# Placing the head-masked low parts of the keys: eight small DMAs per half image in place of copies on GpSimd and VectorE

## The chip, the cores and the metric

One NeuronCore of one Trainium2 chip runs the whole kernel. The metric is the device time of one execution in microseconds (us), lower is better. Three runs of the kernel before gave 392.28, 393.44 and 391.3 us, median 392.28 us.

## The reference, cut to what matters

Eight images of 128 channels and 32x32 pixels go through a Swin-like block (layer norm, attention of 8 heads in windows of 8x8 = 64 tokens, projection, residual, layer norm, a 128-256-128 SiLU network, residual) and then through a linear attention without softmax, which the kernel folds into one 128x128 matrix per image.

```python
normed = _layernorm(win, ln1_g, ln1_b)
q, k, v = jnp.split(normed @ in_w.T + in_b, 3, axis=-1)      # 8 heads of 16
scores = jnp.einsum('bhsd,bhtd->bhst', q, k) / jnp.sqrt(16.)
o = jnp.einsum('bhst,bhtd->bhsd', softmax(scores), v)
win = win + o @ out_w.T + out_b
y = y + silu(_layernorm(y) @ fc1_w.T + fc1_b) @ fc2_w.T + fc2_b
out = wo @ (((wq x + bq) (wk x + bk) / N) (wv x + bv)) + bo + x
```

## The kernel before, in words

The work is cut into 16 half images of 512 tokens (8 windows, 4 pairs of windows), numbered from 0. `Loop.half(c)` is a half, `par` is its parity, and `h.n()` is the count that a semaphore has once half `h` has raised it. Five engine programs are written out by hand in a fixed order and meet only at semaphores. `images` lays them out: a prologue, image 0 (`step_even`, `step_odd`), a hardware loop over images 1 to 6, image 7, an epilogue. One step does the attention of half b (`b_*`), the layer norm and q, k, v of half b+1 (`a_*`), the projection, second layer norm and fc1 of half b-1 (`c_*`), fc2 of half b-2, and in every odd step the last 128x128 matrix of the image before (`d_*`). An engine does its own list strictly in order, so a wait holds all that is queued behind it.

Many products are made in three passes, for precision: a value is split into a high part of type float32r and a low part (the value less its high part), and high*high, high*low and low*high are summed. So q, k, and with them the operands of the scores, exist twice, as `q_h`, `q_l`, `k_h`, `k_l`.

Channels lie on the 128 partitions, 16 per head. The heads are kept apart by zeros: `qd_h` and `qd_l` hold q four times, each copy with the rows of two heads (32 partitions) and zeros elsewhere; `kd_h` and `kd_l` hold k twice, copy 0 with the rows of the even heads and copy 1 with those of the odd heads, zeros in the other rows. All have two slots, by parity.

- `spread_q` on SyncE (L346) fills `qd_h` and `qd_l` with four DMAs each (32 partitions, 2 KB a row); `spread_v` (L361) fills `vd` with four DMAs of 64 partitions and 256-byte runs. SyncE issues every DMA of the kernel, in order: `load_x`, `spread_q`, `spread_v` in each step, and the output at the end of an odd step. It waits for `q_high`, `q_low` and `v_kept` on the way. Zeros are laid once, in the prologue.
- `kd_h` is made on ScalarE (L894) as k_h times a 0/1 column `head_a`.
- `kd_l` is made the same way from `k_l`: copy 0 on GpSimd (`k_low_block`, L457), copy 1 on VectorE (`a_k_low_block`, L1148). As the product writes all 128 rows, no zeros are laid for it.
- TensorE: `b_score` (L611) makes the scores once with the high parts, for the row maxima alone; `b_scoreT` (L629 and L634) makes the transposed scores in three passes, minus the maxima. `b_scoreT(h, 0)` waits for `q_low_dma`, for both `kd_low` and for the widened maxima. `b_attn(h, 0)` (L649) waits for `v_dma`. In the prologue and first step the order of TensorE is: q, k, v of half 0, weights, score(0), score(1), scoreT(0), a_back, score(2), attn(0), q of half 1, scoreT(1), ...
- The next `k_l` (L1140) waits until the copies of the one before are done.
- GpSimd's prologue lays the identity, the zeros and ones of `vd` (L418, L422), then makes the reciprocal deviations of half 0 (L447, L449) on which VectorE's `normalise` (L1105) waits, then zeros of slot 1 of `qd` (L481, L482), then L457.

Of the kernel before, what the change touches and what calls it, by code (L numbers as in the profile page):

```python
# [34 lines left out]
F32 = mybir.dt.float32  # L35
# [87 lines left out]
def build(nc, x, ln1_g, ln1_b, in_w, in_b, out_w, out_b, ln2_g, ln2_b, fc1_w, fc1_b, fc2_w, fc2_b,  # L123
          wq, bq, wk, bk, wv, bv, wo, bo, out):
    ctx = ExitStack()
    with ctx:
# [117 lines left out]
        kd_high, kd_low = sems("kd_high", 2), sems("kd_low", 2)  # L244
# [59 lines left out]
        def _(sp):  # L304
# [55 lines left out]

            def spread_v(h):  # L361
# [17 lines left out]
            def prologue(loop):  # L379
                sp.wait_ge(q_zero_set[0], 2)  # L380
                spread_q(loop.half(0))
                sp.wait_ge(v_const_set, 5)
                spread_v(loop.half(0))
                sp.wait_ge(q_zero_set[1], 2)

            def step_even(loop, more, c):
                if more:
                    load_x(loop.half(2))
                spread_q(loop.half(1))
                spread_v(loop.half(1))  # L390

            def step_odd(loop, more, d):
                if more:
                    load_x(loop.half(3))
                    spread_q(loop.half(2))
                    spread_v(loop.half(2))
# [12 lines left out]
        def _(pool):  # L409
# [7 lines left out]

            pool.memset(vd[:], 0.0).then_inc(v_const_set, 1)  # L418
# [32 lines left out]
            def k_low_block(h):  # L451

                if h.follows(2):
                    pool.wait_ge(scoreT_ready[PAIRS - 1], h.n(2))
                pool.wait_ge(k_low, h.n())
                waited()
                pool.tensor_scalar(kd_l[:, h.par, :, 0, :], k_l[:].bitcast(F32).rearrange("p (win k) -> p win k", k=KEYS),  # L457
                                   head_a[:, 0:1], None, ALU.mult).then_inc(kd_low[0], 1)

# [19 lines left out]
            def prologue(loop):  # L479
# [3 lines left out]
                k_low_block(loop.half(0))  # L483
# [4 lines left out]
            def step(loop, b, with_a, with_next, with_c, with_tail, with_last=False):  # L488
# [5 lines left out]
                if with_a:  # L494
                    residual(a)
                    k_low_block(a)
# [26 lines left out]
        def _(pe):  # L523
# [92 lines left out]
            def b_scoreT(h, p):  # L616

                pe.wait_ge(max_wide_ready[p], h.n())
                if p == 0:
                    pe.wait_ge(q_low_dma, h.n(times=16 * QUADS))  # L620
                    pe.wait_ge(kd_low[0], h.n())
                    pe.wait_ge(kd_low[1], h.n())
# [409 lines left out]
        def _(dve):  # L1032
# [101 lines left out]
            def a_k(h):  # L1134
                dve.wait_ge(k_high, h.n())
                if h.follows(1):
                    dve.wait_ge(kd_low[0], h.n(1))
                if h.follows(1):
                    dve.wait_ge(kd_low[1], h.n(1))
                dve.scalar_tensor_tensor(k_l[:], p_a[1][:], qkv_b[:, 1:2], k_h[:].bitcast(F32),  # L1140
                                         ALU.add, ALU.subtract).then_inc(k_low, 1)

            def a_k_low_block(h):

                if h.follows(2):
                    dve.wait_ge(scoreT_ready[PAIRS - 1], h.n(2))
                dve.wait_ge(k_low, h.n())
                dve.tensor_scalar(kd_l[:, h.par, :, 1, :], k_l[:].bitcast(F32).rearrange("p (win k) -> p win k", k=KEYS),  # L1148
                                  head_a[:, 1:2], None, ALU.mult).then_inc(kd_low[1], 1)
# [117 lines left out]
            def prologue(loop):  # L1267
# [10 lines left out]
                a_k_low_block(a)  # L1278
# [5 lines left out]
            def step(loop, b, with_a, with_next, with_c, with_tail, with_d, with_last=False):  # L1284
# [47 lines left out]
                if with_a:  # L1332
                    a_k_low_block(a)
# [60 lines left out]
```

## Time and profile before

| | |
|---|---|
| runs | 392.28, 393.44, 391.3 us (median 392.28) |
| span of the profiled execution | 389.9 us, first to last instruction; what lies around it is not in the trace, and the median run stands 2.4 us above it |
| TensorE busy | 364.9 us, 94% |
| VectorE busy | 294.5 us, 76% |
| ScalarE busy | 241.8 us, 62% |
| GpSimd busy | 167.4 us, 43% |
| DMA | 31570 packets, 21.94 MB |
| one image in the loop | 44.1 us |

PE is TensorE's matmuls and PEld its weight loads, DVE is VectorE, ACT ScalarE, POOL GpSimd, SP SyncE; SPq rows are DMA issues. A busy PE includes pipelined matmuls that overlap, so it is not PE at its peak. The granted clock is shown as a share of full speed, 1.00 being 2.4 GHz and 0.50 being 1.2 GHz; at the very start, before the first record of the clock, the profile shows 1.00 whatever the matmuls' own durations say.

### The profile page before, as it was taken

How to read it: one execution, taken by the hardware profiler on the slowest of the kernel's cores; microseconds unless marked ns; L12 is line 12 of the kernel's file. 1: busy time of each engine (PE TensorE's matmuls, PEld its weight loads, DVE VectorE, ACT ScalarE, POOL GpSimd, SP SyncE). 2: the span in 40 equal slices, each digit the busy share in tenths (PEclk: the TensorE clock that was granted, in tenths of full speed). 3: DMA queues.
4: the chain of work that ended last, by engine and by line, in shares of the span. 5: the costliest groups of instructions: out<-in, count | busy, mean ns of one | idle time of the engine just before them, and what ended most of it. 6: DMA issues, size and time to landing. Idle time of an engine off the chain costs nothing. (4 is left out here: it accounts for less than half of the span.)

```text
span 389.9 us, 9822 instructions
## 1 busy us (share of the span) xinstructions
PE 364.9 (94%) x3349; PEld 312.5 (80%) x3349; DVE 294.5 (76%) x863; ACT 241.8 (62%) x438; POOL 167.4 (43%) x176
## 2 busy tenths in 40 slices
PE   3679999999999999999999999999999999999874
PEld 2467888888898888888888888888888888888663
DVE  8387888797688768797688868787688868676452
ACT  1426676764959477774958467674858467663540
POOL 6353154454364434544464434544455434441420
PEclk9999999999999999999999999999999999999796
DMA  4223030303222221303122121403122120300101
GB/s 121 40 77 97 23 100 11 102 0 82 73 63 52 49 58 59 102 0 81 58 77 54 46 62 54 108 0 78 57 74 61 40 67 29 79 6 10 45 1 54
DMA packets 31570, 21.94 MB, mean 56 GB/s; under 512 B 22272, under 2 KB 23360, under 8 KB 31552
## 3 DMA queue, kind: packets, MB, share of 16 engines
q1 hardware_dynamic: 31552, 21.71, 20.4%
q8 instruction: 10, 0.16, 0.2%
q14 instruction: 8, 0.07, 0.1%
HBM read 4.92 MB, written 4.19 MB: 23 GB/s over the span
## 5 line engine op out<-in xcount | busy, mean ns | idle before, releaser
L649 PEld LDWEIGHTS p_attn<-vd,probs 128*64 128x64 f32 x1024 | 52.7, 139 | 22.3 <-issue 15.1
L649 PE MATMUL p_attn<-vd,probs 128*64 128x34 f32 x1024 | 62.1, 244 | 2.8 <-ACT probs L910 2.8
L910 ACT ACTIVATE probs<-p_scoreT 128x512 f32<-128x512 f32 x64 | 38.6, 603 | 38.0 <-PE p_scoreT L634 37.5
L465 POOL TENSOR_TENSOR hid_l<-hid,hid_h 128x512 fp32r<-128x512 f32 x30 | 40.4, 1367 | 47.9 <-ACT hid_h L944 45.8
L611 PE MATMUL p_score<-kd_h,qd_h 128*128 128x128 f32 (+1 forms) x512 | 54.6, 249 | 0.8 <-DVE row_max L1158 0.8
L611 PEld LDWEIGHTS p_score<-kd_h,qd_h 128*128 128x128 f32 (+1 forms) x512 | 50.0, 163 | 5.0 <-DVE row_max L1158 1.3
L470 POOL TENSOR_TENSOR y_l<-y,y_h 128x512 fp32r<-128x512 f32 (+1 forms) x17 | 20.6, 1214 | 71.2 <-ACT y_h L924 71.2
L1158 DVE TENSOR_REDUCE row_max<-p_score 128x8 f32<-128x512 f32 x64 | 44.0, 688 | 6.6 <-PE p_score L611 6.6
L634 PE MATMUL p_scoreT<-qd_h,kd_h 128*128 128x256 f32 x128 | 41.3, 322 | 0.0
L457 POOL TENSOR_SCALAR kd_l<-k_l,head_a 128x512 fp32r<-128x512 f32 x16 | 26.7, 1669 | 33.8 <-DVE k_l L1140 20.0
L449 POOL TENSOR_TENSOR rstd<-rstd,minus_half 128x4 f32<-128x4 f32 (+1 forms) x33 | 35.5, 1075 | 2.8
L634 PE MATMUL p_scoreT<-qd_h,kd_l 128*128 128x256 f32 x128 | 36.1, 282 | 0.0
L634 PE MATMUL p_scoreT<-qd_l,kd_h 128*128 128x256 f32 x128 | 36.0, 282 | 0.0
L1105 DVE TENSOR_SCALAR xn_tok<-p_a,mv,rstd 128x128 f32<-128x128 f32 x64 | 21.9, 405 | 13.2 <-POOL rstd L449 13.1
L447 POOL TENSOR_SCALAR rstd<-mv 128x4 f32<-128x4 f32 (+1 forms) x33 | 7.6, 231 | 56.0 <-DVE mv L1097 56.0
L436 POOL TENSOR_SCALAR x_res<-x_in,out_b 128x256 f32<-128x256 f32 x32 | 29.6, 934 | 0.0
L1169 DVE CAST max_wide<-row_max 128x512 bf16<-128x512 f32 x48 | 27.7, 578 | 1.1
L629 PE MATMUL p_scoreT<-neg_ident,max_wide 128*128 128x128 bf16 x256 | 25.2, 221 | 2.0 <-DVE max_wide L1169 2.0
L634 PEld LDWEIGHTS p_scoreT<-qd_l,kd_h 128*128 128x128 f32 x128 | 24.4, 190 | 0.0
L634 PEld LDWEIGHTS p_scoreT<-qd_h,kd_h 128*128 128x128 f32 x128 | 24.3, 190 | 0.0
L634 PEld LDWEIGHTS p_scoreT<-qd_h,kd_l 128*128 128x128 f32 x128 | 24.1, 189 | 0.0
L894 ACT ACTIVATE kd_h<-k_h,head_a 128x512 fp32r<-128x512 f32 x32 | 22.9, 718 | 1.7 <-ACT k_h L887 0.4
(183 smaller groups left out, 881.9 us busy)
## 6 DMA issues: line engine op xcount, KB each, us to landing
x_in<-in_x SPq DMA_DIRECT2D x16, 256.0 KB, 2.8
qd_h<-q_h SPq DMA_DIRECT2D x64, 64.0 KB, 2.0
qd_l<-q_l SPq DMA_DIRECT2D x64, 64.0 KB, 2.0
vd<-v_tok SPq DMA_DIRECT2D x64, 64.0 KB, 2.2
out<-out_sb SPq DMA_DIRECT2D x16, 256.0 KB, 2.0
fc_rows<-in_L_conv_fc_w SPq DMA_DIRECT2D x2, 128.0 KB, 2.6
in_w_rows<-in_L_conv_in_w SPq DMA_DIRECT2D x1, 192.0 KB, 2.7
out_w_rows<-in_L_conv_out_w SPq DMA_DIRECT2D x1, 64.0 KB, 2.5
```

Of the source, the lines that this page charges most:

```text
L436: last = pool.tensor_scalar(in_windows(x_res[:, h.par, :], v), in_rows(x_in[:, h.par, :], v), out_b2[:, 0:1], None, ALU.add)
L449: pool.tensor_tensor(out_[:, tiles], out_[:, tiles], minus_half[:, tiles], ALU.pow).then_inc(out_set, 1)
L457: pool.tensor_scalar(kd_l[:, h.par, :, 0, :], k_l[:].bitcast(F32).rearrange("p (win k) -> p win k", k=KEYS), head_a[:, 0:1], None, ALU.mul ...
L465: pool.tensor_tensor(hid_l[:, t], hid[:, t], hid_h[:, t].bitcast(F32), ALU.subtract).then_inc(hid_low[t], 1)
L611: last = pe.matmul(p_score[0:rows, 2 * KEYS * j:2 * KEYS * (j + 1)], qd_h[:, h.par, j, 2 * KEYS * p:2 * KEYS * p + rows], kd_h[:, h.par, 2 ...
L629: pe.matmul(dst[:, :, j, :], max_wide[:, p % 2, 2 * j:2 * j + 2, :], neg_ident[:], start=j == 0, stop=False, skip_group_check=True)
L634: last = pe.matmul(dst[:, win], kd[:, h.par, window], qd[:, h.par, :, KEYS * window:KEYS * (window + 1)], start=False, stop=win == 1 and k ...
L649: last = pe.matmul(p_attn[64 * win:64 * win + 64, 2 * VB * j:2 * VB * (j + 1)], probs[:, p % 2, win, j, :], vd[:, h.par, 2 * p + win, :, : ...
L894: act.activation(kd_h[:, h.par, :, a, :], k_h[:].bitcast(F32).rearrange("p (win k) -> p win k", k=KEYS), ACT.Copy, scale=head_a[:, a:a + 1 ...
L910: act.activation(probs[:, p % 2], p_scoreT[:].rearrange("row (win j q) -> row win j q", win=2, j=QUADS), ACT.Exp, scale=SCORE_SCALE).then_ ...
L1158: dve.tensor_reduce(row_max[:, p % 2], p_score[:].rearrange("row (h k) -> row h k", h=HEADS), AXIS_X, ALU.max).then_inc(max_ready[p], 1)
L1169: dve.tensor_copy(max_wide[:, p % 2], row_max[:, p % 2].unsqueeze(2).to_broadcast([128, HEADS, KEYS])).then_inc(max_wide_ready[p], 1)
```

## The change

Both halves of `kd_l` are now written by SyncE's DMAs. A new function `spread_k_low` issues one DMA per head, 16 partitions each, from `k_l` to the head's copy of `kd_l`, eight per half image, between `spread_q` and `spread_v`. The two copies on GpSimd and VectorE and their semaphores go. Since the DMAs leave the rows of the other heads alone, GpSimd zeros all of `kd_l` once, at the start, ahead of the zeros of `vd`. TensorE waits for the eight DMAs in place of the two copies.

```diff
+            def spread_k_low(h):
+                sp.wait_ge(k_low, h.n())
+                if h.follows(2):
+                    sp.wait_ge(scoreT_ready[PAIRS - 1], h.n(2))
+                for head in range(HEADS):
+                    rows = slice(DH * head, DH * head + DH)
+                    sp.dma_start(kd_l[rows, h.par, :, head % 2, :].bitcast(F32),
+                                 k_l[rows, :].bitcast(F32).rearrange("p (win k) -> p win k", k=KEYS)
+                                 ).then_inc(kd_low_dma, 16)
...
                 spread_q(loop.half(0))
+                sp.wait_ge(kd_zero_set, 1)
+                spread_k_low(loop.half(0))
                 sp.wait_ge(v_const_set, 5)
                 spread_v(loop.half(0))
...
                 spread_q(loop.half(1))
+                spread_k_low(loop.half(1))
                 spread_v(loop.half(1))
...
                     spread_q(loop.half(2))
+                    spread_k_low(loop.half(2))
                     spread_v(loop.half(2))
...
+            pool.memset(kd_l[:].bitcast(F32), 0.0).then_inc(kd_zero_set, 1)
             pool.memset(vd[:], 0.0).then_inc(v_const_set, 1)
...
-            def k_low_block(h):
...
-                pool.tensor_scalar(kd_l[:, h.par, :, 0, :], k_l[:].bitcast(F32).rearrange("p (win k) -> p win k", k=KEYS),
-                                   head_a[:, 0:1], None, ALU.mult).then_inc(kd_low[0], 1)
...
                     pe.wait_ge(q_low_dma, h.n(times=16 * QUADS))
-                    pe.wait_ge(kd_low[0], h.n())
-                    pe.wait_ge(kd_low[1], h.n())
+                    pe.wait_ge(kd_low_dma, h.n(times=16 * HEADS))
...
                 if h.follows(1):
-                    dve.wait_ge(kd_low[0], h.n(1))
-                if h.follows(1):
-                    dve.wait_ge(kd_low[1], h.n(1))
+                    dve.wait_ge(kd_low_dma, h.n(1, times=16 * HEADS))
...
-            def a_k_low_block(h):
...
-                dve.tensor_scalar(kd_l[:, h.par, :, 1, :], k_l[:].bitcast(F32).rearrange("p (win k) -> p win k", k=KEYS),
-                                  head_a[:, 1:2], None, ALU.mult).then_inc(kd_low[1], 1)
```

The calls of `k_low_block` (GpSimd's prologue and step) and of `a_k_low_block` (VectorE's prologue and step) go with them.

## Rows read from the trace of the kernel before

**Rows 1.** Busy by stretch: us, PE, PEld, DVE, ACT, POOL, clock, DMA share, GB/s.
```profile
188.00:232.00 44.00, 43.76 (x415) 37.86 (x414) 34.95 (x105) 30.06 (x55) 20.41 (x20) 1.00 0.22 59
```
**Rows 2.** Lines L457 and L1148, the two copies: duration in ns, minimum, median, maximum.
```profile
L457 POOL TENSOR_SCALAR kd_l<-k_l,head_a x16: 1567/1570/1841, 17.5 to 335.5; 128x512 fp32r<-128x512 f32 x16
L1148 DVE TENSOR_SCALAR kd_l<-k_l,head_a x16: 476/477/488, 17.3 to 338.6; 128x512 fp32r<-128x512 f32 x16
```
**Rows 3.** Timeline, even step of image 4: start, duration, engine, line, operation, [idle before <-releaser].
```profile
203.73 2.66 SPq L369 DMA_DIRECT2D vd<-v_tok  x4
...
206.87 0.48 DVE L1148 TENSOR_SCALAR kd_l<-k_l,head_a 128x512 fp32r<-128x512 f32 x1
...
208.28 1.37 DVE L1105 TENSOR_SCALAR xn_tok<-p_a,mv,rstd 128x128 f32<-128x128 f32 x4 [0.93 <-POOL rstd L449]
```
**Rows 4.** Timeline, the same halves in the next step, TensorE.
```profile
211.95 0.40 PE L629 MATMUL p_scoreT<-neg_ident,max_wide 128*128 128x128 bf16 x4 [0.24 <-DVE max_wide L1169]
...
215.81 0.97 PE L649 MATMUL p_attn<-vd,probs 128*64 128x34 f32 x16
```
**Rows 5.** Timeline of the prologue and first step, from SyncE's first spreads on.
```profile
16.56 0.75 DVE L1140 SCALAR_TENSOR_TENSOR k_l<-p_a,qkv_b,k_h 128x512 fp32r<-128x512 f32 x1 [0.44 <-ACT k_h L887]
...
17.95 2.49 SPq L358 DMA_DIRECT2D qd_l<-q_l  x4
...
20.54 2.70 SPq L369 DMA_DIRECT2D vd<-v_tok  x4
...
22.12 0.91 PE L611 MATMUL p_score<-kd_h,qd_h 128*128 128x128 f32 x8 [0.78 <-DVE row_max L1158]
...
22.87 0.40 PE L629 MATMUL p_scoreT<-neg_ident,max_wide 128*128 128x128 bf16 x4
...
24.05 0.42 PEld L577 LDWEIGHTS p_a<-ident,xn_tok 128*128 128x128 f32 x4 [0.23 <-DVE xn_tok L1105]
...
26.50 0.97 PE L649 MATMUL p_attn<-vd,probs 128*64 128x34 f32 x16 [0.95 <-ACT probs L910]
```
**Rows 6.** DMA issues on the page: KB each, median us from issue to landing.
```profile
x_in<-in_x SPq DMA_DIRECT2D x16, 256.0 KB, 2.8
...
qd_l<-q_l SPq DMA_DIRECT2D x64, 64.0 KB, 2.0
vd<-v_tok SPq DMA_DIRECT2D x64, 64.0 KB, 2.2
```
**Rows 7.** Issue times in ns of line L320: minimum, median, maximum.
```profile
L320 SPq DMA_DIRECT2D x_in<-in_x x16: 334/386/547, 0.7 to 294.9; - x16
```
**Rows 8.** Timeline, half 1: SyncE in the first step, TensorE in the second.
```profile
34.17 2.65 SPq L369 DMA_DIRECT2D vd<-v_tok  x4
...
40.57 0.40 PE L629 MATMUL p_scoreT<-neg_ident,max_wide 128*128 128x128 bf16 x4
```
**Rows 9.** Timeline, half 15, the last: SyncE, then TensorE.
```profile
337.65 2.65 SPq L369 DMA_DIRECT2D vd<-v_tok  x4
...
344.21 0.40 PE L629 MATMUL p_scoreT<-neg_ident,max_wide 128*128 128x128 bf16 x4 [0.26 <-DVE max_wide L1169]
```
**Rows 10.** Timeline, GpSimd in the prologue.
```profile
2.09 1.91 POOL L418 MEMSET vd<- 128x2176 f32 x1
...
6.58 0.24 POOL L447 TENSOR_SCALAR rstd<-mv 128x4 f32<-128x4 f32 x1 [2.11 <-DVE mv L1097]
```
**Rows 11.** Granted clock by stretch near the end, columns as in the first group.
```profile
365.00:370.00 5.00, 4.54 (x14) 3.63 (x15) 2.14 (x8) 0.57 (x2) 2.76 (x4) 0.51 0.14 52
370.00:375.00 5.00, 4.13 (x28) 3.92 (x27) 3.83 (x8) 2.36 (x6) 1.28 (x2) 0.81 0.01 2
```
**Rows 12.** Timeline, TensorE before and within that stretch.
```profile
363.60 0.44 PE L665 MATMUL p_c<-ident,o_tok 128*128 128x128 f32 x2 [0.26 <-DVE o_tok L1180]
365.01 0.51 PE L529 MATMUL p_c<-o_h,wh 128*128 128x256 f32 x1 [0.98 <-ACT o_h L930]
...
367.75 0.63 PE L529 MATMUL p_c<-hid_l,wh 128*128 128x512 f32 x1
```

More of the change, by code:

```diff
@@ L243, in build @@
         q_high_dma, q_low_dma, v_dma = sem("q_high_dma"), sem("q_low_dma"), sem("v_dma")
-        kd_high, kd_low = sems("kd_high", 2), sems("kd_low", 2)
+        kd_high, kd_low_dma, kd_zero_set = sems("kd_high", 2), sem("kd_low_dma"), sem("kd_zero_set")
         score_ready, max_ready, max_wide_ready = sems("score_ready", 4), sems("max_ready", 4), sems("max_wide_ready", 4)
@@ L449, in rstd @@
                 pool.tensor_tensor(out_[:, tiles], out_[:, tiles], minus_half[:, tiles], ALU.pow).then_inc(out_set, 1)
-            def k_low_block(h):
[L453 to L456, printed above, removed]
-                pool.tensor_scalar(kd_l[:, h.par, :, 0, :], k_l[:].bitcast(F32).rearrange("p (win k) -> p win k", k=KEYS),
-                                   head_a[:, 0:1], None, ALU.mult).then_inc(kd_low[0], 1)
             def hidden_low(h, t):
@@ L482, in prologue @@
                 pool.memset(qd_l[:, 1].bitcast(F32), 0.0).then_inc(q_zero_set[1], 1)
-                k_low_block(loop.half(0))
                 rstd1_of(loop.half(1))
@@ L495, in step @@
                     residual(a)
-                    k_low_block(a)
                 if with_next:
@@ L1136, in a_k @@
                 if h.follows(1):
-                    dve.wait_ge(kd_low[0], h.n(1))
-                if h.follows(1):
-                    dve.wait_ge(kd_low[1], h.n(1))
+                    dve.wait_ge(kd_low_dma, h.n(1, times=16 * HEADS))
                 dve.scalar_tensor_tensor(k_l[:], p_a[1][:], qkv_b[:, 1:2], k_h[:].bitcast(F32),
                                          ALU.add, ALU.subtract).then_inc(k_low, 1)
-            def a_k_low_block(h):
-                if h.follows(2):
-                    dve.wait_ge(scoreT_ready[PAIRS - 1], h.n(2))
-                dve.wait_ge(k_low, h.n())
-                dve.tensor_scalar(kd_l[:, h.par, :, 1, :], k_l[:].bitcast(F32).rearrange("p (win k) -> p win k", k=KEYS),
-                                  head_a[:, 1:2], None, ALU.mult).then_inc(kd_low[1], 1)
             def b_max(h, p):
@@ L1277, in prologue @@
                 a_k(a)
-                a_k_low_block(a)
                 load_weights()
@@ L1331, in step @@
                 b_norm(b, 2)
-                if with_a:
-                    a_k_low_block(a)
                 if with_last:
```

## The prediction

> **What bounds the kernel now.** I read the busy time by stretch first. In one image of the loop TensorE is busy 43.76 of 44 us and no other engine over 35 [rows 1]. So in the loop an edit counts only if it makes TensorE do more or wait. The reader should then not look at what GpSimd and VectorE save, but at the time at which `kd_l` is complete against the time at which TensorE's scoreT(0) of that half wants it. For that I read the timeline, half by half: SyncE's queue on one side, L629 on the other. In the loop much of a step lies between them [rows 3, 4]; in the prologue there is no such distance, since half 0 is used as soon as it is made [rows 5].
>
> **Removed.** Sixteen copies of 1.57 us on GpSimd (25 us) and sixteen of 0.48 us on VectorE (7.6 us) [rows 2]. In a loop step the VectorE copy stands ahead of `xn_tok`, but VectorE still idles 0.93 us after it for GpSimd's rstd [rows 3], which is made from mv, and mv stands ahead of the copy in VectorE's order. So without the copies VectorE only waits longer, 0.93 + 0.48 us. Worth 0. A reason against a hidden gain is TensorE's 0.24 us of idle time per image [rows 1, 4]; all of it, seven times, would be 1.7 us.
>
> **Added on GpSimd.** One memset of 2048 words a partition, ahead of the 2176 of `vd` that took 1.91 us [rows 10]: 1.8 us. GpSimd had idled 2.11 us for VectorE's mv before rstd of half 0 [rows 10], so 0.3 us of cover are left; I take 0. Were it gone, each 0.1 us over would lengthen the prologue by as much.
>
> **Added on SyncE.** Eight DMAs per half between those of q_l and of v. The trace has no DMA of 16 partitions. Nearest in kind are `vd`'s, with 256-byte runs as here: four in 2.65 to 2.70 us, up to 0.68 each; those of q take four in 2.49, 0.62 each [rows 5, 8]. I take a pitch of 0.65, with 0.39 (x_in's issue [rows 7]) and 0.68 as ends. From issue to landing q takes 2.0 and v 2.2 us [rows 6]; half the bytes of either, so 2.1, ends 2.0 and 2.8 (x_in's). The eighth DMA of a half thus starts 7 x 0.65 = 4.55 us after the first and lands 6.65 us after it, and `vd`'s are issued 5.2 us later than now. Their share of the 16 engines is no limit: 0.22 is used in the loop [rows 1], by 12 spreads a half of 64 KB [rows 6] beside the loads and stores; eight of 32 KB add a third to the spreads.
>
> The Trainium skill speaks against this form of transfer: "DMA: Bandwidth & Descriptors", Rules for kernel authors, says that many small transfers should be coalesced and that under 64 KB one pays mostly overhead. The trace agrees so far as 64 KB in 2.0 us and 256 KB in 2.8 us show [rows 6]. The page's fit for one DMA on another issue path (2.0 us plus bytes over 436 GB/s) would put 32 KB at an estimated 2.1 us, the same as I took.
>
> **Where that meets TensorE, half by half.** The first of the new DMAs can go when q_l's are issued, which is where `vd`'s first stands now; k_l is there by then (in the prologue at 17.31 us [rows 5]).
> - Half 0: 20.54 + 6.65 = 27.2 us, and scoreT(0) began at 22.87 [rows 5]. TensorE waits 4.3 us more. Behind the wait stand a_back, score(2) and attn(0), and for them ScalarE's a_xn and VectorE's row maxima, so nothing fills it. Given back: a_back had waited 0.23 us for `xn_tok` [rows 5], which is early now. With the ends: 20.54 + 7 x 0.39 + 2.0 = 25.3, a wait of 2.4; or 20.54 + 7 x 0.68 + 2.8 = 28.1, a wait of 5.2. `vd`: first issue 25.74, fourth 27.8, landed 30.0; attn(0) would come at 26.50 + 4.1 = 30.6 [rows 5], so it is not held, by 0.6 us.
> - Half 1 (both sides shifted alike): 34.17 + 6.65 = 40.8 against 40.57 [rows 8]: 0.25 us, ends 0 and 1.2.
> - Even steps of the loop: 203.73 + 6.65 = 210.4 against 211.95: 1.5 us to spare. `vd` would land at 203.73 + 5.2 + 3 x 0.68 + 2.2 = 213.2 against 215.81: 2.6 to spare [rows 3, 4]. An odd step has the `d_*` work besides and leaves more room. Worth 0.
> - Half 15: 337.65 + 6.65 = 344.3 against 344.21 [rows 9]: 0.1 us, ends 0 and 1.1.
>
> **The clock.** TensorE would stand still from 22.12 + 0.91 = 23.0 [rows 5] to 27.2 us. In the trace of before its clock fell to the 1.2 GHz level at the end of the kernel, at a point where it had been idle for 0.98 us after a gap of 0.26: the stretch 365 to 370 has 0.51 and the next 0.81, so it was slow for some 7 us [rows 11, 12]. An idle time of four microseconds is far longer, so I expect the fall here, after which the first step's TensorE work runs at half pace until the clock is back. Seven slow microseconds do the work of 3.5: the cost has the ends 0 (no fall, or all under waits for ScalarE) and 3.5. I take 1.5, below the middle of the two, since about a microsecond of it lies under the wait for `probs` (0.95 us [rows 5]) and one case says little of how long the next spell is.
>
> The Trainium skill, "TensorE: Matmul & The Clock Gate", HAM oscillation, tells of the same: a wait for a DMA that is long enough puts the array back to half rate, and the next work starts cold. By that rule the fall is all but certain; the single case of rows 11 and 12 agrees.
>
> **The sum.** 4.3 - 0.2 + 1.5 + 0.25 + 0.1 = 5.95 us on a span of 389.9, so 395.8, and as the same 2.4 us lie around it, 392.28 + 5.95 = 398.2 us.
>
> **Rivals.**
> 1. The clock stays up or its fall is covered: 392.28 + 4.45 = 396.7 us. For it: the stage has other engines' waits to hide in, as 0.95 us before attn(0) [rows 5]. Against: rows 11 and 12.
> 2. The new DMAs go out faster, as x_in's do: the wait of half 0 is 2.4, halves 1 and 15 cost nothing, and so short a gap may leave the clock: 392.28 + 2.2 = 394.5. For it: x_in's 0.39 [rows 7]. Against: 256-byte runs cost 0.66 to 0.68 in the nearest rows [rows 5, 8].
> 3. The loop's even steps are late too, because a 16-partition DMA costs more than any seen, or lands late when eight are queued. It decides from a pitch of 0.65 + 1.5/7 = 0.87 us. At 1.0: 2.45 us more in half 0, half 1 and half 15, and 1.0 in each of 6 even steps: 398.2 + 7.4 + 6 = about 411.
> 4. The other side: faster. If a step's length were set by VectorE's chain and not by TensorE, the 0.48 us off VectorE in each half after the first [rows 2] would come back, 15 x 0.48 = 7.2 us, against the 5.95 lost: 391.0; with the 2.2 of rival 2 it is 387.3. It decides from 0.4 us per half. Against it: 43.76 of 44 busy [rows 1] and the 0.93 us of idle time right behind the copy [rows 3].
>
> That the change isn't what it says can be put aside: all five orders are written out by hand.
>
> **How the numbers follow.** Forecast with a fall of the clock 0.52 (its own range 396.5 to 400.5), rival 1 0.25, rival 2 0.10, rival 3 0.07, rival 4 0.06. Within 0.5% (2 us, about what a measurement of this kernel can tell from no change) lies half of rival 4 and some of rival 2's lower edge: 0.07. Faster by more: 0.04. Slower by more: 0.89. Range: from rival 2's 394.5 to 401.5, the forecast with a full fall of the clock (5.95 + 2 for the 3.5, and 1.3 for pitch and landing); rival 3 and rival 4 are left out.
>
> **What would show it.** In the timeline of the changed kernel L629 of half 0 starts at about 27.2 us, released by a DMA of `kd_l`; the eight issues take 5.2 us; if the clock fell, the matmuls of 512 columns (L529) that follow take 0.63 us each, as in the slow stretch [rows 12]; an image of the loop takes as long as before. I am wrong if the period of an image changes, if the issues have another pitch, or if scoreT(0) of a loop step waits for a DMA.

## The result: 401.3 us against 392.3, and where the 9 us lie

The changed kernel takes 401.31 us (median of 4 runs, 401.2 to 403.37), the kernel before 392.27 us beside it (391.3 to 393.44). The ratio is 1.0249, 95% interval 1.021 to 1.0287: slower by 9.0 us, where 5.95 were forecast. The profiled execution has a span of 399.6 us against 389.9, so 9.7 us are to be found between the two traces.

First the page of the changed kernel: its busy times, the wait of TensorE's transposed scores, and the new transfers.

```profile
PE 366.4 (92%) x3349; PEld 314.3 (79%) x3349; DVE 286.8 (72%) x847; ACT 242.1 (61%) x438; POOL 140.6 (35%) x161
...
DMA packets 50002, 26.15 MB, mean 65 GB/s; under 512 B 40704, under 2 KB 41792, under 8 KB 49984
...
L638 PE MATMUL p_scoreT<-qd_h,kd_l 128*128 128x256 f32 x128 | 36.3, 284 | 0.0
...
L633 PE MATMUL p_scoreT<-neg_ident,max_wide 128*128 128x128 bf16 x256 | 25.2, 221 | 9.2 <-DMA kd_l<-k_l 6.2
...
kd_l<-k_l SPq DMA_DIRECT2D x128, 32.0 KB, 2.1
```

GpSimd's busy time fell from 167.4 to 140.6 us and VectorE's from 294.5 to 286.8, for the most part the copies that are gone. It bought nothing. TensorE idles 9.2 us ahead of L633 (L629 before), 6.2 of them for `kd_l`. The same line's query says in how many places, and what an issue and a landing take (ns, then us):

```profile
L368 SPq DMA_DIRECT2D kd_l<-k_l x128: 599/600/1655, 20.6 to 349.8; - x128
...
  PE p_scoreT L633: 6.2, 3
...
DMA to landing us min/median/max: 2.1/2.1/3.1
```

Three waits, then, of 4.32, 1.46 and 0.44 us (halves 0, 1 and 2): 6.2 us, not 9.7. To find the rest I set the starts of TensorE's scoreT(p) of every half of the two traces side by side (64 pairs) and looked at where their distance grows. The timeline of the changed kernel, prologue and first step, answers [rows 5]:

```profile
20.56 5.19 SPq L368 DMA_DIRECT2D kd_l<-k_l  x8
22.15 0.90 PE L616 MATMUL p_score<-kd_h,qd_h 128*128 128x128 f32 x8 [0.79 <-DVE row_max L1152]
...
25.85 2.67 SPq L380 DMA_DIRECT2D vd<-v_tok  x4
27.37 0.59 PE L633 MATMUL p_scoreT<-neg_ident,max_wide 128*128 128x128 bf16 x4 [4.32 <-DMA kd_l<-k_l]
...
31.98 0.97 PE L653 MATMUL p_attn<-vd,probs 128*64 128x34 f32 x16 [0.90 <-ACT probs L914]
...
33.69 0.40 PE L633 MATMUL p_scoreT<-neg_ident,max_wide 128*128 128x128 bf16 x4
```

scoreT(0) went from 22.87 to 27.37 (+4.50), scoreT(1) from 28.20 to 33.69 (+5.49). The further microsecond is the clock, in the columns of [rows 1]; over the same 28 to 32 us the kernel before had 1.00:

```profile
24.00:28.00 4.00, 0.63 (x5) 0.66 (x6) 1.17 (x3) 0.00 (x0) 2.35 (x3) 0.50 0.29 59
28.00:32.00 4.00, 3.10 (x19) 2.95 (x18) 0.88 (x2) 1.77 (x6) 0.00 (x0) 0.67 0.41 115
```

Half 1 answers [rows 8]. SyncE is through with q_l 5.5 us later than before, as TensorE is with its work, but its eight issues take 6.20 us and not 5.19, and TensorE waits:

```profile
39.67 6.20 SPq L368 DMA_DIRECT2D kd_l<-k_l  x8
...
45.92 2.62 SPq L380 DMA_DIRECT2D vd<-v_tok  x4
47.61 0.38 PE L633 MATMUL p_scoreT<-neg_ident,max_wide 128*128 128x128 bf16 x4 [1.46 <-DMA kd_l<-k_l]
```

Half 2 is the first that the hardware loop uses. The kernel before, then the changed one:

```profile
51.80 3.29 SPq L369 DMA_DIRECT2D vd<-v_tok  x4
59.28 0.40 PE L629 MATMUL p_scoreT<-neg_ident,max_wide 128*128 128x128 bf16 x4 [0.25 <-DVE max_wide L1169]
```

```profile
58.76 5.60 SPq L368 DMA_DIRECT2D kd_l<-k_l  x8
66.06 0.38 PE L633 MATMUL p_scoreT<-neg_ident,max_wide 128*128 128x128 bf16 x4 [0.44 <-DMA kd_l<-k_l]
```

From SyncE's free place to TensorE's use there were 7.5 us here, where image 4 has 8.2 [rows 3, 4]. One of the eight issues took 1.07 us, and a loop step did wait for its DMAs.

Half 9, made in the even step of image 4 and used in the odd one, answers [rows 3, 4]:

```profile
211.03 5.15 SPq L368 DMA_DIRECT2D kd_l<-k_l  x8
...
215.47 1.37 DVE L1109 TENSOR_SCALAR xn_tok<-p_a,mv,rstd 128x128 f32<-128x128 f32 x4 [1.24 <-POOL rstd L465]
...
218.06 1.11 DVE L1163 CAST max_wide<-row_max 128x512 bf16<-128x512 f32 x1
219.41 0.38 PE L633 MATMUL p_scoreT<-neg_ident,max_wide 128*128 128x128 bf16 x4 [0.42 <-DVE max_wide L1163]
```

Here no DMA is waited for. VectorE's idle time before `xn_tok` grew from 0.93 to 1.24 us. But TensorE's wait for `max_wide` is 0.42 us where it was 0.24, though the CAST takes 1.11 us in both. That small difference comes back in every odd half of the loop. (In the even halves from 4 on TensorE has no such wait: for half 8 the CAST takes 0.43 us in both kernels and is done 0.3 us before its use. Half 2 is like the odd halves: the CAST took 1.12 us in the kernel before, and TensorE waited 0.25.) An image of the loop shows it in TensorE's busy time (43.76 before [rows 1]):

```profile
152.00:196.00 44.00, 43.58 (x412) 37.62 (x411) 34.21 (x102) 29.90 (x54) 16.75 (x18) 1.00 0.28 70
```

The account of the 9.7 us, by that distance (forecast terms beside it):

| where | measured | forecast |
|---|---|---|
| half 0, wait and clock | +5.47 | 4.3 - 0.2 + 1.5 |
| half 1 | +1.13 (1.57, of which 0.4 comes back within the step) | 0.25 |
| halves 2 to 15 | +1.31: 0.16 in half 2, 0.17 to 0.21 in each odd half from 3 to 13, 0.08 in half 15, nothing in the even ones from 4 on | 0.1 |
| behind scoreT(3) of half 15 | +1.76 (31.44 to 33.20 us) | 0 |

Half 0 came as forecast. The other three are what the experiments are about.

### The profile page after: what moved, and what is told of

It is laid out like the page before. It is cut to its first block and busy times, and to the rows that moved or that the text cites. A ratio compares the mean times of both kernels' runs of the same rounds, so it can differ in the third digit from the quotient of the medians.

```text
span 399.6 us, 9915 instructions
## 1 busy us (share of the span) xinstructions
PE 366.4 (92%) x3349; PEld 314.3 (79%) x3349; DVE 286.8 (72%) x847; ACT 242.1 (61%) x438; POOL 140.6 (35%) x161
## 5 line engine op out<-in xcount | busy, mean ns | idle before, releaser
L465 POOL TENSOR_TENSOR rstd<-rstd,minus_half 128x4 f32<-128x4 f32 (+1 forms) x33 | 33.7, 1021 | 2.8
L633 PE MATMUL p_scoreT<-neg_ident,max_wide 128*128 128x128 bf16 x256 | 25.2, 221 | 9.2 <-DMA kd_l<-k_l 6.2
L633 PEld LDWEIGHTS p_scoreT<-neg_ident,max_wide 128*128 128x128 bf16 x256 | 16.6, 98 | 15.0 <-issue 13.0
L1163 DVE CAST max_wide<-row_max 128x512 bf16<-128x512 f32 x48 | 25.9, 540 | 1.1
```

The source lines that it names most:

```text
L465: pool.tensor_tensor(out_[:, tiles], out_[:, tiles], minus_half[:, tiles], ALU.pow).then_inc(out_set, 1)
L633: pe.matmul(dst[:, :, j, :], max_wide[:, p % 2, 2 * j:2 * j + 2, :], neg_ident[:], start=j == 0, stop=False, skip_group_check=True)
L1163: dve.tensor_copy(max_wide[:, p % 2], row_max[:, p % 2].unsqueeze(2).to_broadcast([128, HEADS, KEYS])).then_inc(max_wide_ready[p], 1)
```

## The experiments

Each was timed beside the kernel before, on the same chip as it (its medians there 391.73 to 391.81 us). "Shift" is the distance of TensorE's scoreT(3) from that of the first trace of the kernel before; "end" is the time behind scoreT(3) of half 15, 31.44 us there.

### Half 0 and the clock

**Half 0 by the engines.** Theory: the eight DMAs of half 0 alone cost 5.5 us. GpSimd and VectorE make `kd_l` of half 0 as before, the DMAs all others.

```diff
                 spread_q(loop.half(0))
                 sp.wait_ge(kd_zero_set, 1)
-                spread_k_low(loop.half(0))
...
+                k_low_block(loop.half(0))
...
+                a_k_low_block(a)
```

> The changed kernel, but the low parts of half 0 alone are made by GpSimd and VectorE as before the change; the eight DMAs serve halves 1 to 15. Theory A (the largest part of the loss is the wait of TensorE for half 0's DMAs and the fall of its clock behind it, 5.5 us between scoreT(0) of half 0 and scoreT(1) of half 0 in the two traces): L629's first start returns to 22.9 us, the clock is not at 0.50 between 24 and 31 us, and the time is 401.3 - 5.5 = 395.8 us. Theory B (the loss is in the loop, by the added DMA traffic or by the waits on it, and what the prologue loses is made up later): no more than 1 us is gained, 400.3 us or more.

Measured: 393.9 us (10 runs), ratio 1.0068 (1.0038 to 1.0097), 7.4 us under the changed kernel. More than expected, for two reasons that the trace shows: half 1 adds nothing at scoreT(3), and the end is 0.49 us shorter than in the trace of before, 2.25 us shorter than in that of the changed kernel. The DMAs of half 1 are late here too: TensorE waits 0.32 us for them, which comes back within the half, since TensorE is 2.0 us later than before and SyncE only 0.9 (35.10 against 34.17). In half 2 it waits 0.63 us for them. Halves 2 and 3 add 0.39 and 0.32 us, the odd halves from 5 to 13 add 0.15 to 0.22. The half-0 shift is still 2.0: the clock fell in this execution too, though TensorE waited for no DMA:

```profile
28.00:32.00 4.00, 4.00 (x22) 3.40 (x23) 3.05 (x8) 1.29 (x2) 0.00 (x0) 0.57 0.09 22
```

**Both kernels once more.** How much of the half-0 shift belongs to the kernel, and how much to the execution? The two kernels unchanged, each profiled again.

> The kernel before, unchanged, for a second trace. Theory A (the end of the kernel behind scoreT(3) of half 15, 31.4 us in the first trace and 33.2 in the changed kernel's, differs from execution to execution with the places where the clock falls, and the 1.8 us are not the change's): the end is another length here, by half a microsecond or more, and the clock falls elsewhere. Theory B (the end is fixed for a kernel): 31.4 us again.

> The changed kernel, unchanged, for a second trace, with the same question as for the kernel before. Theory A: the end is not 33.2 us, and with it what half 0 loses to the clock (1.0 us in the first trace) may differ; scoreT(0) of half 0 starts at 27.4 us again, and each odd step is 0.17 us longer again. Theory B: 33.2 us again.

Measured: the kernel before, span 391.56 us (393.37 us), had a shift of 2.15 us in the first step, then nothing to the last half, and an end 0.44 us shorter (half a microsecond was asked of theory A). The changed one, span 399.59 (401.4 us), nearly repeated its first trace: shifts 5.46, 6.26 and 8.01 at halves 0, 1 and 15, end +1.69. Half 2 alone differs, 0.65 us in place of 0.16, with a wait of 0.92 us for its DMAs. The 2.15 us of the kernel before are the clock:

```profile
28.00:32.00 4.00, 4.00 (x23) 3.44 (x22) 3.08 (x8) 1.29 (x2) 0.00 (x0) 0.57 0.08 20
```

So the kernel before loses up to 2.15 us in its first step in some executions, and the trace that I predicted from was one without that loss. TensorE's longest wait there in this trace is the 0.95 us for `probs` before attn(0). Here the clock fell without a wait of four microseconds. The Trainium skill ("TensorE: Matmul & The Clock Gate", HAM oscillation) ties the fall to long waits for DMAs; that agrees with half 0 of the changed kernel, and does not describe this fall.

**Half 0 kept busy.** To price the clock alone: 32 matmuls into an unread bank stand ahead of scoreT(0) in the first step of the changed kernel, so that TensorE does not stand still. They are extra work, used by nothing.

```diff
+                if not with_c:
+                    for _ in range(32):
+                        pe.matmul(p_c[0][:, 0:2 * C], wh[:, 0, :], wh[:, 0:2, :], start=True, stop=True)
```

> The changed kernel with 32 matmuls of 256 columns more, on constant operands and into an unused bank, between score(1) and scoreT(0) of half 0, where TensorE waits for the DMAs. They fill 23.0 to 26.8 us at the full clock and delay nothing. Theory A (of the 5.5 us lost in half 0, 1.0 is the clock, which falls while TensorE waits): the granted clock stays 1.00 in the first step, scoreT(1) of half 0 follows scoreT(0) by 5.3 and not by 6.3 us, and about 1.0 us is gained, 400.3 us, if the end of the kernel doesn't change. Theory B (the 1.0 us is not the clock but the order of the work behind the wait): the distance stays 6.3 us and the time 401.3 us.

Measured: 401.39 us, ratio 1.024 (1.019 to 1.029): nothing gained, where 1.0 us was expected. The profiled execution shows what happened in it. The clock did stay up,

```profile
24.00:28.00 4.00, 3.30 (x28) 3.10 (x26) 1.52 (x4) 0.00 (x0) 2.71 (x3) 1.00 0.21 38
...
20.54 6.55 SPq L368 DMA_DIRECT2D kd_l<-k_l  x8
...
28.73 0.38 PE L633 MATMUL p_scoreT<-neg_ident,max_wide 128*128 128x128 bf16 x4 [1.43 <-DMA kd_l<-k_l]
```

and from scoreT(0) to scoreT(1) it took 5.08 us (28.73 to 33.81) instead of 6.32 in the changed kernel. The clock thus costs 1.24 us of half 0. But SyncE's eight issues took 6.55 us in this execution and scoreT(0) began 1.36 us later, which took it away. Whether that holds for the other three runs is not known. What follows from the trace: clock 1.2 us, wait 4.5, and a late DMA can eat the one if the other is won.

**Four of the eight from ScalarE.** If SyncE's issue pitch sets half 0, two queues halve it. ScalarE issues heads 4 to 7 of half 0.

```diff
-                for head in range(HEADS):
+                for head in range(HEADS if h.follows(1) else HEADS // 2):
...
+                for head in range(HEADS // 2, HEADS):
+                    rows = slice(DH * head, DH * head + DH)
+                    act.dma_start(kd_l[rows, 0, :, head % 2, :].bitcast(F32),
```

> The changed kernel, but of half 0's eight DMAs four are issued by ScalarE, idle at that time, and four by SyncE; halves 1 to 15 as in the change. Theory A (the wait of half 0 is the length of SyncE's queue, eight issues of 0.65 us, and a landing of 2.1): the last of them lands 4 x 0.65 = 2.6 us earlier, L629's first start is at 24.8 instead of 27.4 us, and as TensorE idles 1.8 us and no longer 4.3 the clock may stay up: 2.6 to 3.7 us gained, 397.6 to 398.8 us. Theory B (the sixteen DMA engines or the landing are the limit, not the issue): scoreT(0) starts at 27 us as before and the time is 401 us.

Measured: 398.01 us, ratio 1.0175 (1.0132 to 1.0219), 3.3 us under the changed kernel.

```profile
18.41 2.67 ACTq L979 DMA_DIRECT2D kd_l<-k_l  x4
20.80 2.61 SPq L368 DMA_DIRECT2D kd_l<-k_l  x4
...
25.05 0.43 PE L633 MATMUL p_scoreT<-neg_ident,max_wide 128*128 128x128 bf16 x4 [1.30 <-DMA kd_l<-k_l]
```

The wait of 4.32 us fell to 1.30 and scoreT(0) from +4.50 to +2.18. The two queues have about the same pitch (2.67 and 2.61 us for four); ScalarE starts 2.4 us before SyncE and is through 0.3 us after SyncE's first has started. The clock fell here too (0.66 in 24:28, 0.92 in 28:32), and the shift of half 0 is 3.0 us in place of 5.5. The profiled execution was the fastest of the four (396.16 us), and its end is 2.5 us shorter than in the changed kernel's trace (mean granted clock 0.88 against 0.79), so not all of the gain in time is the queue's.

### The DMAs or the wait: the rest of the loop

**The DMAs, read by nobody.** The kernel before, its copies kept, with the eight DMAs of each half added into a tile that nothing reads. It costs whatever SyncE's queue and the DMA engines cost, without TensorE's wait for `kd_l` (VectorE still waits for these DMAs before it writes the next `k_l`).

```diff
+        kd_x = sb("kd_x", [C, 2, WH, 2, KEYS], F32R)
...
+                    sp.dma_start(kd_x[rows, h.par, :, head % 2, :].bitcast(F32),
```

> The kernel before with the eight DMAs per half added at the same place of SyncE's order, but into a tile that nobody reads; kd_l is still made by GpSimd and VectorE and TensorE waits for these. It prices SyncE's queue alone. Theory A (the queue costs where what stands behind it is wanted at once): scoreT(0) of half 0 stays at 22.9 us, but the DMAs of v are issued 5.2 us later, so attn(0) of half 0 starts at about 30.1 instead of 26.5 us, with a fall of the clock behind it: 4 to 5 us in half 0, nothing in the loop: 396.5 to 398 us. Theory B (only the wait on kd_l costs): attn(0) is not held and the time is 392.3 to 393 us.

Measured: 395.75 us, ratio 1.0106 (1.0064 to 1.0148). From half 1 to half 15 the shift does not move, to 0.02 us: neither the queue, nor the packets, nor later `vd` cost the loop anything. All of the loss lies in half 0, +5.87 us, and there it is now `v` that is late, behind the eight issues. The time is only 4.0 us longer, and below the 396.5 expected, since the end of this execution is 1.85 us shorter than in the trace of before (mean granted clock 0.94 there against 0.77).

```profile
25.78 2.67 SPq L380 DMA_DIRECT2D vd<-v_tok  x4
...
30.14 1.50 PE L663 MATMUL p_attn<-vd,probs 128*64 128x34 f32 x16 [3.92 <-DMA vd<-v_tok]
```

**The copies, read by nobody.** The other side: the changed kernel with the 32 copies put back, into a tile that nothing reads.

```diff
+                pool.tensor_scalar(kd_x[:, h.par, :, 0, :], k_l[:].bitcast(F32).rearrange("p (win k) -> p win k", k=KEYS),
...
+                dve.tensor_scalar(kd_x[:, h.par, :, 1, :], k_l[:].bitcast(F32).rearrange("p (win k) -> p win k", k=KEYS),
```

> The changed kernel with the two copies put back on GpSimd and VectorE at their old places, into a tile that nobody reads: it prices what the change takes away. Theory A (the copies were hidden, as the prediction said): distances in the loop and time are the changed kernel's, 401.3 us within 1 us. Theory B (the copies cost something in each step, and the change loses in spite of a gain there): the loop is longer by up to 0.4 us a half, and the time goes to 403 us or more.

Measured: 400.28 us, ratio 1.0218 (1.0191 to 1.0244), 1.0 us under the changed kernel, within the spread of both. The whole time can't price the copies, since the clock differs in the trace: it stays low longer in the first step (0.70, 0.50 and 0.52 in 24:28, 28:32 and 32:36), which makes half 0 1.6 us longer than in the changed kernel, and the end is 29.80 us in place of 33.20 (mean granted clock 0.94 against 0.79). The loop is that of the changed kernel: 0.15 to 0.24 us in odd halves, 0.40 in half 2 (a wait of 0.65 us for its DMAs), 0 in the later even ones. So in the loop 25 us of GpSimd and 7.6 us of VectorE are worth nothing either way, as forecast.

```diff
+                kd_count = h.n(times=16 * HEADS) if p == 0 else None
...
-                    pe.wait_ge(kd_low_dma, h.n(times=16 * HEADS))
+                    pe.wait_ge(kd_low_dma, kd_count)
```

> The changed kernel, but TensorE's sequencer works out the count for its wait on the DMAs of kd_l ahead of the wait for the widened maxima, not behind it. Theory A (the 0.18 us by which each odd step of the loop is longer is this register operation, which stands between the wait for the maxima and the first weight load): the two traces' scoreT(0) keep their distance through the loop, the 0.18 us of halves 3, 5, ... 13 go, and 1.0 to 1.2 us are gained: 400.2 us. Theory B (the 0.18 us come of the DMAs themselves, by landing late or by their traffic): nothing changes, 401.3 us.

Measured: 400.79 us, ratio 1.0229 (1.0166 to 1.0293), odd halves 0.16 to 0.22 us. It is no test: in the instruction records the register operation still stands where it stood, with the wait for `max_wide` on it, and the weight load that begins the scores comes two sequencer steps later. In image 4 these are: the register operation with the wait for `max_wide` (218.75, 32 ns), the wait for the DMAs (218.85, 51 ns), the weight load (218.92); in the changed kernel they stand at 219.21, 219.31 and 219.38, with the same durations. In the kernel before the weight load itself carried the wait for `max_wide` (211.94).

**The kernel before with such a count.** VectorE's copy raises its semaphore by 3 instead of 1, and TensorE waits for three times the count. Nothing else: no DMA is added, none is waited for.

```diff
-                                  head_a[:, 1:2], None, ALU.mult).then_inc(kd_low[1], 1)
+                                  head_a[:, 1:2], None, ALU.mult).then_inc(kd_low[1], 3)
...
-                    pe.wait_ge(kd_low[1], h.n())
+                    pe.wait_ge(kd_low[1], h.n(times=3))
```

> The kernel before with one thing of the change alone: TensorE's wait for kd_l has a count of its own (VectorE's copy counts 3 in place of 1), so that the loop needs a register operation for it, behind the wait for the widened maxima. No DMA is added and both copies stay. Theory A: each odd step is 0.18 us longer, 1.1 to 1.3 us over the kernel, 393 us. Theory B: no difference in the loop, 391.7 us.

Measured: 393.82 us (10 runs), ratio 1.0032 (1.0007 to 1.0058). The odd halves from 3 to 13 grow by 0.16 to 0.19 us and half 2 by 0.16, as in the changed kernel. Halves 1 and 15, which lie outside the hardware loop, where the count is a constant, grow by 0.01 and not at all. TensorE's waits between 28 and 350 us, total, times and longest, first of the kernel before, then of this one:

```profile
PE p_scoreT L629 <- DVE max_wide L1169: 2.0, 8, 0.3
```

```profile
PE p_scoreT L629 <- DVE max_wide L1169: 3.2, 8, 0.4
```

The same eight waits, 1.2 us longer, with not one DMA more. (Its first step also has a shift of 1.57 us: the clock fell, as in the second trace of the kernel before.)

**The wait for the maxima put last.** If it is the work between the late wait and the first weight load, it should vanish when the late wait comes last. In the changed kernel:

```diff
             def b_scoreT(h, p):
-                pe.wait_ge(max_wide_ready[p], h.n())
...
                     pe.wait_ge(probs_ready[p - 1], h.n())
+                pe.wait_ge(max_wide_ready[p], h.n())
```

> The changed kernel, but in b_scoreT TensorE's wait for the widened maxima stands last of the waits, not first. In e2 the register operation had not moved: it still carried the wait for the maxima, and one more wait stood between it and the first weight load. Here it runs before that wait. Theory A (register operation and wait behind the maxima are the 0.18 us of each odd step): halves 3, 5, ... 13 lose nothing to the kernel before, the shift at scoreT(3) of half 15 is smaller by 1.1 to 1.3 us than in the changed kernel (7.9), about 6.7, and the time is 400.1 us. Theory B (the 0.18 us come of something else, the missing copies or the DMAs): the shift stays 7.9 and the time 401.3 us.

Measured in the trace: the odd halves from 3 to 13 fell to 0.06 to 0.09 us and the shift at half 15 from 7.91 to 7.04. Of these 0.87 us the loop and half 15 give 0.55; the rest is half 1, which added 0.65 us here, and half 0, which lost 0.16 more. The expected 6.7 was not reached, as some of the odd halves' loss stays. The wait of image 4 is 0.33 us:

```profile
218.81 0.38 PE L633 MATMUL p_scoreT<-neg_ident,max_wide 128*128 128x128 bf16 x4 [0.33 <-DVE max_wide L1163]
```

The time did not follow: 402.11 us, ratio 1.0263 (1.0235 to 1.029). The profiled span is 0.8 us shorter than that of the changed kernel, the median 0.8 longer; the profiled execution was the fastest of the four (400.54 us), and its end is 1.80 us over that of before. The cause of the odd halves is shown by the pair of kernels (it comes with the count alone, and more than half of it goes with the order alone); that mending it makes the kernel faster is not shown.

**Both put right.** Halves 0 and 1 by the engines, DMAs from half 2 on, the wait for the maxima last as in the run before.

```diff
-                spread_k_low(loop.half(0))
...
-                spread_k_low(loop.half(1))
+                if loop.half(1).follows(2):
+                    spread_k_low(loop.half(1))
...
-                    pe.wait_ge(kd_low_dma, h.n(times=16 * HEADS))
+                    if h.follows(2):
+                        pe.wait_ge(kd_low_dma, h.n(2, times=16 * HEADS))
+                    else:
+                        pe.wait_ge(kd_first[0], h.n())
+                        pe.wait_ge(kd_first[1], h.n())
```

> The changed kernel with each cause found so far taken out: the low parts of halves 0 and 1 are made by GpSimd and VectorE as before the change, and TensorE waits for the maxima last. The eight DMAs serve halves 2 to 15. Theory A (the wait of half 0 with its clock, the wait of half 1, and the register operation are the whole loss): scoreT(0) of half 0 at 22.9 us, no wait for a DMA of kd_l, 0.07 us left in each odd step, and a time within 1 us of the kernel before, 391.7 to 392.7 us. Theory B (the loop loses something yet, to the DMAs): over 393 us. It isn't expected to be faster than the kernel before, since TensorE has no idle time in the loop that the DMAs could give back.

Measured: 392.99 us (390.63 to 396.42, 10 runs), ratio 1.0012 (0.9971 to 1.0052). This lies between what the two theories asked. Shift 0.70 at halves 0 and 1 (the clock fell, 0.83 in 20:24 and 0.75 in 24:28), 0.06 to 0.08 added in each odd half from 3 to 13, 1.27 at half 15; TensorE waits for no DMA of `kd_l`, and the end is 31.07 us. With DMAs in 14 of the 16 halves the kernel can't be told from the one before, nor is it faster. Three things changed together against the changed kernel (halves 0 and 1, the order of the waits, and with them the end, 2.1 us shorter), so this run doesn't say which of them the time came from. By the account above, the first two halves are 6.6 of the 9.7 us.

### The end

The end behind half 15 grew by 1.76 us though it has no `kd_l` in it. The granted clock is below 1.00 in the end of both kernels [rows 11], at other places in each; its mean over the end is 0.77 before and 0.79 after. To take the clock out, 27 matmuls into an unread bank are spread over the gaps of the epilogue, the same in both kernels:

```diff
+                def busy(n):
+                    for _ in range(n):
+                        pe.matmul(p_score[:, 0:2 * C], wh[:, 0, :], wh[:, 0:2, :], start=True, stop=True)
+
+                pe.wait_ge(max_ready[PAIRS - 1], 2 * IMAGES)
...
                 c_transpose(late)
+                busy(4)
                 c_project(late)
+                busy(2)
```

> The kernel before with 27 matmuls of 256 columns more in the epilogue, on constant operands and into an unused bank, at the places where TensorE waits there (0.4 to 1.3 us each). Theory A (the end is as long as the clock makes it): the granted clock stays 1.00 to the last matmul, the last six matmuls take 0.4 and not 0.63 us each, and the end behind scoreT(3) of half 15 shrinks from 31.4 us to 28 to 30, which would put this kernel 1 to 3 us under the kernel before. Theory B (the end is a chain of other engines): no gain, or a loss of up to 1 us, as the fillers stand in TensorE's way.

> The changed kernel with the same 27 matmuls in its epilogue. Theory A (the 1.8 us by which its end is longer are the clock's): its end is now as long as that of the kernel before with the same addition, within 0.3 us, and 3 to 5 us shorter than its 33.2. Theory B (the 1.8 us are the change's own): its end stays 1.8 us longer than the other's.

Measured: the kernel before 390.86 us (10 runs), ratio 0.9967 (0.9941 to 0.9993); the changed one 398.55 us, ratio 1.0185 (1.0123 to 1.0248). The clock stays at 1.00 to the last matmuls in both, and the last matmuls of 512 columns take 0.40 us in place of 0.63. The ends are 28.62 and 29.46 us, 2.8 and 3.7 us shorter than without the filling: they differ by 0.84, no longer by 1.76, and not by under 0.3 as theory A asked. So by these traces about 0.9 us of the 1.76 were the clock; as its mean was no lower in the changed kernel's end, it is a matter of where the slow stretches lay. The times fell by less than the ends, 0.9 and 2.8 us; the profiled execution of the filled kernel before lost 2.0 us in its first step, where the clock fell. The other 0.84 have a place of their own. VectorE's `hid_l` and GpSimd's `y_l` in the epilogue, first the kernel before, then the changed one, both filled:

```profile
376.40 0.43 DVE L1268 TENSOR_TENSOR hid_l<-hid,hid_h 128x256 fp32r<-128x256 f32 x1 [0.81 <-ACT hid L959]
377.13 0.43 DVE L1268 TENSOR_TENSOR hid_l<-hid,hid_h 128x256 fp32r<-128x256 f32 x1 [0.30 <-ACT hid L959]
377.42 0.72 POOL L470 TENSOR_TENSOR y_l<-y,y_h 128x256 fp32r<-128x256 f32 x1 [4.06 <-ACT y_h L937]
377.70 0.36 PE L529 MATMUL p_c<-hid_h,wh 128*128 128x256 f32 x1 [0.63 <-DVE hid_l L1268]
```

```profile
382.40 0.43 DVE L1262 TENSOR_TENSOR hid_l<-hid,hid_h 128x256 fp32r<-128x256 f32 x1 [0.81 <-ACT hid L963]
383.43 0.72 POOL L477 TENSOR_TENSOR y_l<-y,y_h 128x256 fp32r<-128x256 f32 x1 [4.06 <-ACT y_h L941]
383.49 0.94 DVE L1262 TENSOR_TENSOR hid_l<-hid,hid_h 128x256 fp32r<-128x256 f32 x1 [0.66 <-ACT hid L963]
384.57 0.36 PE L534 MATMUL p_c<-hid_h,wh 128*128 128x256 f32 x1 [1.50 <-DVE hid_l L1262]
```

Where VectorE starts first, `hid_l` takes 0.43 us; where GpSimd starts 0.06 us ahead, it takes 0.94, and TensorE waits 1.50 us instead of 0.63: 0.87 us, which is the 0.84 but for 0.03. `hid_l` takes 0.94 us there in the changed kernel, in its second trace and in four variants of it (the number first, kept busy, wait order, four from ScalarE), and 0.42 in both traces of the kernel before, in its variants, with half 0 by the engines, with the unused copies and with both put right. The Trainium skill ("SBUF — State Buffer", Who interferes with whom) says that a VectorE instruction with two inputs in SBUF contends with a GpSimd one that reads SBUF, calls the contention for the ports that they share an exclusive lock, and says that the order of issue decides which of the two blocks. The rows agree for VectorE as the later one (its 0.94 us are the 0.66 that `y_l` still had to go and 0.28 more), and not for GpSimd: its 0.72 us are the same in both orders. That `y_l` is first in the one group is VectorE's doing: `y_l` starts 1.02 us after the first `hid_l` in both traces, but the second `hid_l` starts 0.73 us after the first in the one and 1.09 in the other, though ScalarE's `hid` that it reads ends 0.64 us after it in both (377.04 and 383.04). So VectorE starts 0.36 us late, for a reason that the rows don't show. With half 0 by the engines the same 0.36 us stand ahead of the first `hid_l` (1.16 us idle in place of 0.80), where they cost nothing. What delays VectorE is open. It is not the copies' absence alone, since with the DMAs in all halves but the first the second `hid_l` is quick.

## Why the prediction was partly wrong

- **Half 0: right.** The pitch was 0.65 us as assumed (eight in 5.19), the landing 2.1, scoreT(0) at 27.37 against 27.2, 4.50 us later than before against 4.3. Moving four of the eight off the queue took 2.3 us of it away. `vd` was early enough there, as said (attn(0) waited for `probs`).
- **The clock: right in kind and near in size.** 1.5 were assumed, 1.0 is in the account and 1.24 by the run that kept it up (the 0.2 given back lie between the two). The sign named for it did not show: the matmuls of 512 columns came at 32.88 us, when the clock was back, and took 0.50, 0.39 and 0.40 us, about as before; the fall shows in the granted clock (0.50, then 0.67) and in the 0.59 us of scoreT(0)'s first rows. What the sum left out is that the kernel before can have such a loss too. In its second trace it has 2.15 us. Since the medians of before lie near the first trace's 392.28 us, this moved the forecast little, but a single trace did not show it.
- **Memset on GpSimd: 0, right.** TensorE's score rows of half 0 stand within 0.03 us of before up to 22.15 us.
- **The removed copies: 0, right.** VectorE waits longer for rstd instead (0.93 to 1.24 us, where 1.41 was worked out), and 32 unused copies put back left the loop as it was.
- **Half 1: mis-sized, 1.13 us against 0.25.** The step was "34.17 + 6.65 = 40.8 against 40.57". The distance was right, but from the first issue to scoreT(0) it took 7.94 us (39.67 to 47.61), 1.1 more than in half 0 (20.56 to 27.37), and here there was no cover for it. In this trace one of the eight issues took 1.655 us in place of 0.6 (6.20 us for the eight). That is not the whole of it: with half 0 by the engines and with the unused copies the eight issues of half 1 had their usual length (5.18 and 5.13 us), and scoreT(0) still began 7.90 and 7.78 us after the first. So in these traces half 1's DMAs are about a microsecond late with or without a slow issue; why stays open. The end of that term (1.2) was put into the range, its likeliest value was not. Slow issues are in the trace of before as well, and I had not looked for them: 3 of 244 there, 5 of 372 in the changed kernel (last section).
- **The loop: the failed step.** "Worth 0" was right of the DMAs in all but the first loop step: half 9 has 1.7 us to spare (211.03 + 6.65 against 219.41, where 1.5 were worked out), and the unused DMAs left the loop as it was, to 0.02 us. It was read from image 4 alone. Half 2 has less (51.80 + 6.65 = 58.45 against 59.28 in the trace of before, 0.8 us), and there TensorE waited 0.44 us for a DMA, 0.92 in the second trace, at a net price of 0 to 0.5 us. The larger error is another. "Worth 0" was wrong of the edit: I weighed when the awaited thing is complete, and did not cost the wait itself. Two waits against a count in a register became one against a count that is computed, and TensorE's sequencer does that after its late wait and before the first weight load: 0.17 to 0.21 us in every odd half of the loop, 1.1 us in six of them and 1.3 in halves 2 to 15. Two of the prediction's own tests, "if the period of an image changes" and "if scoreT(0) of a loop step waits for a DMA", were met. Rows that could have warned were there: the 0.24 us before scoreT(0) [rows 4] say that this place has no slack.
- **The end: the other failed step.** The sum took everything behind half 15 as unchanged. It grew by 1.76 us: about 0.9 by where the clock was low, 0.84 by a late start of VectorE and the order of `hid_l` and `y_l`, whose cause stays open.
- **The rivals.** 1 (clock up) is refuted: it fell. 2 (pitch 0.39) is refuted by the pitch of 0.65. 3 did not come as described (the pitch is not 0.87 or more), but single slow issues did make one loop step late. 4, faster by VectorE's chain, is refuted: the loop did not get shorter in any kernel.

The sum with the measured terms is 4.5 + 1.0 (half 0) + 1.1 + 1.3 + 1.8 = 9.7 us. The forecast's 5.95 is short by 0.9 (half 1), 1.2 (loop) and 1.8 (end). The direction and the largest term held, the size did not: 9.0 us are one and a half times the forecast. The median of 401.31 us lies at the very edge of the range (401.5), the ratio put on the 392.28 us of before (402.0 us) lies past it, and the forecast's own range, 396.5 to 400.5, holds neither.

## What to carry to other kernels

A DMA that takes the place of a copy is free only where the pipeline has distance; cost the first passes by themselves, where the issue pitch times the count lies bare (here eight times 0.65 us), and leave these to the engines. Cost the wait as well as what is waited for: a count that has to be computed, behind the wait that ends last, is paid each time on the engine that bounds the kernel, and in the traces most of that price goes when the wait that ends last stands behind all others (in the time this could not be shown). And take more than one trace of the kernel before, since its own losses to the clock (0 to 2.15 us in one step) were as large as a term of the sum.

## What the runs showed of the hardware that was not expected

- **Slow DMA issues.** The packet records show a 16 KB packet of the instruction queue beside every issue of SyncE over 0.9 us: before at 52.5 us (1280 ns), 89.7 (1672) and 334.7 (2226), after at 44.2 (1655), 59.4 (1068), 84.1 (972), 96.6 (1238) and 342.5 (1985), each within 0.5 us of such a packet. It is a coincidence in time, 8 of 8; the reverse does not hold, as each trace has ten such packets; no run tested it.
- **A wait on a computed count costs TensorE 0.16 to 0.21 us** where it stands behind the late wait (kernel before with a count times three: 0.16 to 0.19), and 0.06 to 0.09 us are left when the late wait comes last.
- **The clock in the kernel before.** It fell between 27.4 and 28.4 us in three traces (its second one, its variant with the count times three, its variant with the end filled), each with no wait of TensorE over 1 us there, and not at all there in the first one. Filling the epilogue's gaps kept it up at the end and gave 390.86 us, ratio 0.9967 (0.9941 to 0.9993), the fastest kernel of the study, by about 1 us.
- **18432 packets more, all under 512 bytes,** cost the loop nothing: in the kernel with the unread DMAs the share of the DMA engines in the loop went from 0.22 to 0.28, and no half came later.
